# Fixed SBUF homes for the attention's queries, keys and values; the first batch loaded from the projection phase, in loads of 16 rows

## The reference, cut to what matters

```python
def _L0_attn_ref(x, Wqa, Wqb, Wkva, Wkvb, Wout, bout):   # after a layer norm; 8 batches of 512 tokens, 256 wide
    H, KVH = (16, 4)                                      # D = 16
    q = (x @ Wqa @ Wqb).reshape(b, s, H, D)
    kv = (x @ Wkva @ Wkvb).reshape(b, s, KVH, D, 2)
    k, v = (kv[..., 0], kv[..., 1])
    q, k = _rope(q), _rope(k)
    ...
    scores = jnp.einsum('bqhd,bkhd->bhqk', q, k) * scale  # k, v repeated over 4 heads; causal mask
    w = jax.nn.softmax(scores, axis=-1)
    out = jnp.einsum('bhqk,bkhd->bqhd', w, v).reshape(b, s, E)
    return out @ Wout + bout
x = x + _L0_attn_ref(_layernorm(x), ...)
x = x + _L0_xattn_ref(_layernorm(x), ctx_1024, ctx_1024, ...)   # 8 x 64 context rows, 16 heads of 64, and an MLP
x = x + _L0_ffn_ref(_layernorm(x), ...)                         # ternary weights
```

## Time and profile before

| | us |
|---|---|
| median of 3 runs | 1288.27 |
| lowest and highest | 1285.8, 1289.26 |
| the profiled execution | 1285.26 |
| its span, first to last instruction | 1283.3 |

### The profile page before, as it was taken

The page is one execution under the profiler, slowest core; times in us unless marked ns, Lnnn a source line. Parts: engine busy times, 40 slices in busy tenths (PEclk is TensorE's granted clock), DMA queues, the critical chain, the costliest instruction groups (busy, mean ns, idle before and its releaser), DMA issues. The chain is left out here.

```text
span 1283.3 us, 23288 instructions
## 1 busy us (share of the span) xinstructions
PE 1041.0 (81%) x7133; PEld 759.8 (59%) x7133; DVE 800.5 (62%) x1737; ACT 648.8 (51%) x1155; POOL 369.8 (29%) x516
## 2 busy tenths in 40 slices
PE   3777148888899997488257999999999999998997
PEld 2444013334444442478246787978878787886986
DVE  3888546567777772576246565656756565766554
ACT  1333205456666666455133647465564746546554
POOL 0333326567433333101031213122211222221110
PEclk9777658889999999699677999999999999999999
DMA  2332323334222210336711211212101121010000
GB/s 90 100 118 90 113 98 104 109 107 125 95 93 92 90 42 34 126 140 263 268 50 49 80 38 66 67 65 65 65 17 49 65 65 65 16 64 2 18 1 33
DMA packets 52994, 103.89 MB, mean 81 GB/s; under 512 B 6656, under 2 KB 32768, under 8 KB 48832
## 3 DMA queue, kind: packets, MB, share of 16 engines
q1 hardware_dynamic: 49756, 95.62, 22.0%
q0 software_dynamic: 1920, 6.03, 1.6%
q10 hardware_dynamic: 1252, 1.39, 0.4%
HBM read 63.05 MB, written 39.58 MB: 80 GB/s over the span
## 5 line engine op out<-in xcount | busy, mean ns | idle before, releaser
L803 ACT ACTIVATE p_probs<-p_psS 128x512 f32<-128x512 f32 (+1 forms) x352 | 181.0, 564 | 123.6 <-ACTq L802 121.3
L705 DVE CUSTOM_DVE_ANT_0 p_psA<-p_psA,p_mask 128x512 f32<-128x512 f32 (+1 forms) x256 | 155.6, 647 | 104.4 <-DVEq L703 104.1
L1856 DVE TENSOR_TENSOR p_hl<-p_h,p_hh 128x512 fp32r<-128x512 f32 x128 | 100.9, 791 | 119.9 <-DVEq L1855 119.0
L837 PE MATMUL p_psA<-p_ks,p_qs 96*128 96x512 bf16 (+3 forms) x512 | 144.7, 318 | 35.4 <-PEq L835 34.9
L1674 ACT ACTIVATE p_h<-p_psG,w_columns 128x512 f32<-128x512 f32 x128 | 88.2, 689 | 128.5 <-ACTq L1673 127.6
L856 PE MATMUL p_psS<-p_qs,p_ks 99*128 99x256 bf16 (+3 forms) x512 | 131.8, 311 | 21.2 <-PEq L881 12.3
L724 POOL TENSOR_SCALAR_AFFINE_SELECT p_probs<-p_probs 128x512 f32<-128x512 f32 x128 | 80.7, 634 | 133.1 <-POOLq L723 113.9
L867 PE MATMUL p_psO<-p_probs,p_v 128*32 128x512 f32 (+3 forms) x1024 | 93.3, 460 | 25.1 <-PEq L863 24.4
L2140 PE MATMUL p_psY<-p_n,p_hh 128*128 128x256 f32 x512 | 106.8, 292 | 7.9 <-PEq L2131 4.5
L856 PEld LDWEIGHTS p_psS<-p_qs,p_ks 99*128 99x128 bf16 x512 | 44.0, 99 | 107.9 <-issue 93.2
L2140 PEld LDWEIGHTS p_psY<-p_n,p_hh 128*128 128x128 f32 x512 | 86.2, 196 | 15.9 <-issue 14.7
(11 more groups left out here) (260 smaller groups left out, 2744.0 us busy)
## 6 DMA issues: line engine op xcount, KB each, us to landing
p_n<-n_parts SPq DMA_DIRECT2D x16, 1024.0 KB, 6.8
o_sums<-p_o SPq DMA_DIRECT2D x32, 256.0 KB, 3.0
n_parts<-p_nh SPq DMA_DIRECT2D x8, 1024.0 KB, 3.9
n_parts<-p_nl SPq DMA_DIRECT2D x8, 1024.0 KB, 6.1
q_parts<-p_part SPq DMA_DIRECT2D x48, 128.0 KB
p_qs<-q_parts SPq DMA_DIRECT2D x32, 192.0 KB
p_x<-in_x_dram SPq DMA_DIRECT2D x8, 512.0 KB, 4.2
p_qs<-q_parts SPq DMA_DIRECT2D x32, 128.0 KB
```

Source lines behind the costliest of these rows:

```text
L705: nc.vector.tensor_tensor_reduce(out=bank[:, 0:w], in0=bank[:, 0:w], in1=mask[:, S - w:S], scale=1.0, scalar=MASKED, op0=ALU.add, op1=ALU.max,
L803: nc.scalar.activation(probs[:, g % 2, at:at + n * w], psS[place(s, turn) % SB][:, 0:n * w], ACT.Exp, scale=SCALE).then_inc(exp_done, 1)
L837: last = nc.tensor.matmul(bank[:, z * w:(z + 1) * w], qs[0:SROWS, k, g * G + r0 + z, i * P:(i + 1) * P], ks[0:SROWS, k, g, 0:w], start=Tru ...
L1856: nc.vector.tensor_tensor(hl[:, s, :], h[:, s, :], hh[:, s, :].bitcast(F32), ALU.subtract).then_inc(h_parts, 1)
```

## The change

44 KB per partition of SBUF, three tensors, are allocated ahead of all phases: `home0` for `qs` (32 KB), `home1` for `ks` (8 KB), `home2` for `v` (4 KB). The later phases lay tiles of their own onto them (`nh`, `nl`, `k`, `k2` in the preparation; `q`, `rows`, `sq`, `o` in the mixing), instead of allocating them apart. In the profile of the changed kernel these tiles are all called `home`.

`load_queries` and `load_keys` are functions of the module. They issue one DMA for each of the six blocks of 16 rows, six where there were three, and none has a broadcast source. This holds for every load of the attention, not only the first.

In the projection, SP's stores of the third pair (`stores(B - 4 + k, k, True)`) are followed, unit by unit, by loads of batch 0 into the home: behind units 0 to 3 the queries of groups 0 to 3, behind units 4 and 5 the two halves of the keys and values. The phase ends with a wait for them. In the attention ACT raises the semaphores of the first batch by hand and loads the keys of the second batch alone; SP issues all queries of the second batch ahead of `maxima(0, 0)`.

```diff
+def load_queries(queue, scr, qs, b, k, g, landed):
+    heads = slice(g * G, (g + 1) * G)
+    for row, (pq, _) in enumerate(PAIRS):
+        queue.dma_start(qs[row * D:(row + 1) * D, k, heads, :].rearrange("p h t -> p (h t)"),
+                        scr["q"][pq, :, b, heads, :].rearrange("d h t -> d (h t)")).then_inc(landed, 16)
+
+def load_keys(queue, scr, ks, v, b, k, z, landed):
+    two = slice(z * KVH // 2, (z + 1) * KVH // 2)
+    for row, (_, pk) in enumerate(PAIRS):
+        queue.dma_start(ks[row * D:(row + 1) * D, k, two].rearrange("p g t -> p (g t)"),
+                        scr["k"][pk, b, :, two].rearrange("d g t -> d (g t)")).then_inc(landed, 16)
+    queue.dma_start(v[:, k, two].rearrange("p g t n -> p (g t n)"),
+                    scr["v"][b].rearrange("p (z n) -> p z n", z=2)[:, z]).then_inc(landed, 16)
...
+            def first_batch(n):
+                if n < KVH:
+                    load_queries(sp, scr, qs0, 0, 0, n, first_in)
+                else:
+                    load_keys(sp, scr, ks0, v0, 0, 0, n - KVH, first_in)
...
+                    if ahead:
+                        first_batch(n)
...
-                stores(B - 4 + k, k)
+                stores(B - 4 + k, k, True)
...
+            sp.wait_ge(first_in, 16 * (KVH * len(PAIRS) + 2 * (len(PAIRS) + 1)))
...
-                    if first and g + 1 < KVH:
-                        load_queries(1, 1, g + 1)
...
             for g in range(KVH):
-                load_queries(0, 0, g)
+                load_queries(sp, scr, qs, 1, 1, g, q_in[1][g])
             maxima(0, 0)
-            load_queries(1, 1, 0)
...
-            for k in range(2):
-                for z in range(2):
-                    load_keys(act, k, k, z)
+            for g in range(KVH):
+                act.sem_inc(q_in[0][g], 16 * len(PAIRS))
+            for z in range(2):
+                act.sem_inc(kv_in[0][z], 16 * (len(PAIRS) + 1))
+            for z in range(2):
+                load_keys(act, scr, ks, v, 1, 1, z, kv_in[1][z])
```

More of the change, by code:

```diff
@@ L204, in load, with stores @@
                 sp.dma_start(x[:, k], a["x"][b].rearrange("(t p) f -> p t f", p=P)).then_inc(x_in[k], 16)
-            def stores(b, k):
+            def first_batch(n):
[3 more added lines that the diff above has]
+                    load_keys(sp, scr, ks0, v0, 0, 0, n - KVH, first_in)
+            def stores(b, k, ahead=False):
                 sp.wait_ge(v_ready, 1)
@@ L608, in attend_phase @@
         block = ctx.enter_context(nc.Block())
-        def load_keys(queue, b, k, z):
-            two = slice(z * KVH // 2, (z + 1) * KVH // 2)
-            row = 0
-            for pq in range(PARTS):
-                n = sum(p == pq for p, _ in PAIRS)
-                rows = slice(row * D, (row + n) * D)
-                queue.dma_start(ks[rows, k, two].rearrange("p g t -> p (g t)"),
-                                scr["k"][0:n, b, :, two].rearrange("i d g t -> i d (g t)")).then_inc(kv_in[k][z], 16)
-                row += n
-            queue.dma_start(v[:, k, two].rearrange("p g t n -> p (g t n)"),
-                            scr["v"][b].rearrange("p (z n) -> p z n", z=2)[:, z]).then_inc(kv_in[k][z], 16)
         @block.sync
@@ L626, in _ @@
                 sp.dma_start(dst, src).then_inc(loaded, 16)
-            def load_queries(b, k, g):
-                heads = slice(g * G, (g + 1) * G)
-                row = 0
-                for pq in range(PARTS):
-                    n = sum(p == pq for p, _ in PAIRS)
-                    rows = slice(row * D, (row + n) * D)
-                    sp.dma_start(qs[rows, k, heads, :].rearrange("p h t -> p (h t)"),
-                                 scr["q"][pq, :, b, heads, :].rearrange("d h t -> d (h t)").unsqueeze(0).broadcast_to([n, D, G * S])
-                                 ).then_inc(q_in[k][g], 16)
-                    row += n
             def maxima(k, g):
@@ L1387, in _, with mix_phase @@
             pe.sem_inc(MN_free, -MN_BANKS)
-def mix_phase(nc, a, scr, w, out):
+def mix_phase(nc, a, scr, w, q, rows, sq, o, out):
     with ExitStack() as ctx:
@@ L1433, in mix_phase @@
         minus = signs[:, 0:1]
-        o = sb("o", [P, C, S], F32)
         oh, ol = sb("oh", [P, C, S], F32R), sb("ol", [P, C, S], F32R)
         xin = sb("xin", [P, TT, E], F32)
-        x1 = sb("x1", [P, TT, E], F32)
-        q0 = sb("q0", [P, TT, E], F32)
+        x1, q0, base, x1b = rows
         z = sb("z", [P, TT, E], F32)
-        base = sb("base", [P, TT, E], F32)
-        x1b = sb("x1b", [P, TT, E], F32)
         x2 = sb("x2", [P, TT, E], F32)
@@ L2296, in decoder_block @@
            "rden": dram("rden", [B, H, S]), "n": dram("n_parts", [B, 2, P, XT * E])}
-    project_phase(nc, a, scr)
     with ExitStack() as ctx:
+        homes = [ctx.enter_context(nc.sbuf_tensor(f"home{i}", [P, n], F32))[:, :]
+                 for i, n in enumerate((H * S, KVH * S, 2 * KVH * TT * 2 * D))]
+        qs = homes[0].bitcast(BF16).rearrange("p (k h t) -> p k h t", k=2, h=H)
+        ks = homes[1].bitcast(BF16).rearrange("p (k g t) -> p k g t", k=2, g=KVH)
+        v = homes[2].rearrange("p (k g t n) -> p k g t n", k=2, g=KVH, t=TT)
+        half = H * S // 2
+        nh, nl = (homes[0][:, i * half:(i + 1) * half].bitcast(F32R).rearrange("p (z t n) -> p z t n", t=XT, n=E)
+                  for i in range(2))
+        q = homes[0][:, 0:half].rearrange("p (t s) -> p t s", t=XT)
+        rows = [homes[0][:, half + i * half // 4:half + (i + 1) * half // 4].rearrange("p (t n) -> p t n", t=TT) for i in range(4)]
+        sq = homes[1].rearrange("p (i s) -> p i s", s=S)
+        k, k2 = homes[1].rearrange("p (i n) -> p i n", i=2), homes[2]
+        o = homes[2].rearrange("p (c t) -> p c t", c=C)
+        project_phase(nc, a, scr, qs, ks, v)
         w = mixing_weights(nc, ctx)
@@ L2304, in decoder_block @@
             cw = context_weights(nc, until_n)
-            attend_phase(nc, a, scr, split_list(a, w, cw), split_sems)
-            prepare_phase(nc, a, scr, w, cw)
-        mix_phase(nc, a, scr, w, out)
+            attend_phase(nc, a, scr, qs, ks, v, split_list(a, w, cw), split_sems)
+            prepare_phase(nc, a, scr, w, cw, nh, nl, k, k2)
+        mix_phase(nc, a, scr, w, q, rows, sq, o, out)
 def mixing_weights(nc, ctx):
```

29 lines of the change are left out of this document (11 added, 18 removed).

## The result

The changed kernel takes **1252.06 us** (median; 1251.53 to 1255.04), the kernel before 1287.94 beside it on the same chip: a ratio of 0.973, with a 95% interval of 0.971 to 0.975. The forecast was 1270 with a range down to 1259, so the sign was right and the gain was nearly twice what was forecast. The profiled execution has a span of 1249.7 us against 1283.3, 33.6 us less, where 18.4 were expected.

The account below looks back on a forecast made before the run. The prediction took SP's issuing to bound the projection's end and a DMA backlog on two engines to hold up the attention; 4.6 - 16.0 - 7.0 = -18.4 us gave 1266.9, stated as a 1270 us median, range 1259 to 1282.

Parts of the forecast that it names:

- 38 loads in the projection: End of projection: 19.0 us of SP issuing less 14.4 us idle, so the phase ends 4.6 us later (0.8 to 13.7).
- p: What one 16-row load costs SP, issue and gap: taken as 0.50 us, bounds 0.40 and 0.74.
- The start of the attention: First batch: no wait for maxima, DVE's fill late next, column scores at T + 23.9 instead of T + 39.9: 16.0 us gained.
- Later groups: Groups after the first column scores: less refill backlog, 5.1 us of waits, 1.3 of clock, 0.6 of shorter waits; 7.0 gained.
- bound of half the excess: Later groups: upper bound 14.2 us, half of the 28.4 us by which seventeen groups exceed the pitch without refills.
- more comes back: Rival for the later groups: clock and POOL's gaps both follow the backlog, 14.2 us gained there, 1263 us; chance 0.16.
- SP in the loop: Key refills in the attention loop: SP ends 1.2 us before the next maxima, so no cost while p stays under 0.55.
- Nothing: ACT's 14 loads instead of 16 at the start and the homes' changed addresses: no effect on time.
- The rival that SP becomes the bound: Projection and loop: SP's load issues delay both; at p = 0.74 18 us slower, 1306 us; chance 0.04.
- The prediction's sentence on sizes: Attention loads: 96 and 128 KB become 64 and keys become 32, against a page calling transfers under 64 KB descriptor-dominated.
- The loads don't spread: Rival for the attention: 16-row loads drain like the old ones, maxima again need 14.9 us, 1285 us; chance 0.05.

Follow-up runs that it names:

- the shape alone: Kernel before with every attention load of queries and keys as six 16-row DMAs; nothing loaded early, no shared homes: 1250.63 us, ratio 0.972.
- the merged loads: Changed kernel with pairs reordered, so a group's queries are three DMAs of 48, 32 and 16 rows without a broadcast; keys stay six: 1247.63 us, ratio 0.969.

## Why the prediction was wrong

Step by step, as the prediction has them.

1. **38 loads in the projection**: forecast +4.6, measured +5.6. The mechanism held, p was 0.46 instead of 0.50, and nearly all of SP's idle time was used up. The last stores are issued 4.9 us later (147.76 to 152.65), and the rest is the way from them to T, 4.8 instead of 4.1.

2. **The start of the attention**: column scores at T + 23.9 forecast, T + 24.9 measured, with no wait for the maxima, the fill late next, and the maxima issued at T + 18.6 instead of T + 17.4. The first maximum came at T + 9.2, 1.3 later than the forecast T + 7.95, because the fill itself ran 1.4 us later after T. That there are 14 idle engines to spread over was right. What was wrong is how much they carry: 380 GB/s was scaled up from two engines' 24 each, and sixteen moved 230 at a share of 0.99, 14 each. It did no harm here since the maxima had six microseconds of room; in the start without the early batch, where PE waits at a share of 1.05, it counts. The backlog of before was also not SP's twelve query loads alone, as the prediction has it: of the 146 packets between 186.0 and 191.6 us, 73 were SP's and 73 ACT's, whose key loads of the old shape were issued until 176.2.

3. **Later groups**: forecast -7.0 with bounds 0 and 14.2, measured **-24.2**, of which 23.0 lie in the first seventeen groups. This is the step that failed, and its bound failed with it. The rows above split the 23.0 by the prediction's own terms:

   | in the seventeen groups, us | before | after | difference | predicted |
   |---|---|---|---|---|
   | PE's waits for the rows of maxima (L881, now L885) | 7.7 | 2.8 | -4.9 | -5.7 |
   | PE's busy time, same matmuls (the granted clock) | 149.5 | 139.5 | **-10.0** | -1.3 |
   | PE's waits for masked tiles (L863, now L867) | 16.3 | 7.6 | **-8.7** | 0 |
   | PE's waits for ACT's tiles | 0.6 | 1.2 | +0.6 | 0 |

   What the prediction read from SP's rows, the maxima behind the backlog, it sized rightly. It put POOL's waits at nothing ("POOL's 3.02 us gap ahead of it stays"), with no reason but that they were POOL's, and the clock at 1.3 us, read from one stretch of 6.8 us; the 8.25 us at the lower level behind PE's wait of 8.34, a wait that it took away itself, are in no term. Its bound of half the excess has no reason beside it, other than "Part of that is POOL's". The excess itself, 28.4, holds the wait of 3.5 us at 241.43 twice, since one piece ends with that column score and the other begins with the issue of the maxima before it; from column score to column score (191.75 to 371.46) seventeen groups exceed the pitch by 24.8, and half of that is 12.4. The split was not far off: without POOL's weight pieces, 13.3 of the 24.3 us were gone, 55%. But POOL's share was late for the same reason as SP's. Its pieces wait for their own DMAs, and those were late whenever loads of the old shape were in the queues: the third row below, 5.6 us, was 5.8 and 5.5 in the two runs with old loads and is 4.0 and 3.8 in the changed kernel and with the shape alone. DMA issues of the kernel before, POOL's (KB each, median us from issue to landing):

```profile
p_stage<-in_L_xattn_wk_dram POOLq DMA_DIRECT2D x4, 256.0 KB, 6.1
p_stage<-in_L_xattn_wv_dram POOLq DMA_DIRECT2D x4, 256.0 KB, 5.7
p_stage<-in_L_xattn_w_dram POOLq DMA_DIRECT2D x4, 256.0 KB, 5.6
p_stage<-in_L_xattn_w_dram POOLq DMA_DIRECT2D x8, 128.0 KB, 4.2
```

   The same of the kernel after, and of the kernel before with the pieces behind the groups, where little else is queued (the last row):

```profile
p_stage<-in_L_xattn_wk_dram POOLq DMA_DIRECT2D x4, 256.0 KB, 3.2
p_stage<-in_L_xattn_wv_dram POOLq DMA_DIRECT2D x4, 256.0 KB, 3.9
p_stage<-in_L_xattn_w_dram POOLq DMA_DIRECT2D x4, 256.0 KB, 4.0
p_stage<-in_L_xattn_w_dram POOLq DMA_DIRECT2D x8, 128.0 KB, 3.0
...
p_stage<-in_L_xattn_w_dram POOLq DMA_DIRECT2D x8, 128.0 KB, 2.3
```

   POOL works in order, so a piece that waits keeps the next mask waiting, and PE's wait for the mask was read as POOL's own slowness. The rival "more comes back" named the right mechanism (clock and POOL's gaps both follow the backlog) and gave it 0.16, but took its size from the same half. Half of the excess comes back with the refills' shape and half with that of the first two batches' loads, and the run with old refills says which half is which. The refills' 10.5 us (162.04 - 151.50) are 8.7 of waits for masked tiles and 2.5 of clock, less 0.6 of waits for ACT's tiles; the other 12.4 (174.47 - 162.04) are 7.5 of clock and 4.9 of waits for maxima, and no wait for POOL. Not settled is how much the clock would have cost by itself: the idle stretches and the lower level came and went together in these runs, so they can't be taken apart.

4. **SP in the loop**: forecast nothing, with 1.2 us of room. Right: 0.86 us of room, p 0.455, and the maxima 9.09 apart.

5. **Nothing** for the homes and ACT's loads, and preparation and mixing as long as before: right, 774.4 us each.

The rival that SP becomes the bound needed p of 0.64; the slowest six loads of 16 rows took 0.57 each, once, and those in the loop 0.455. The prediction's sentence on sizes, beside this rival, misreads them: a group's queries were loads of 192, 128 and 64 KB and became 64, and the 96 and 64 KB are the keys', which became 32. "The loads don't spread" was wrong in both its parts.

**How many engines, and how large a transfer.** The DMA share was 0.12 and 0.13 while the copies and parts of the old shape drained, 0.99 with loads of 16 rows, and 0.94 with the merged loads, which have the old sizes and a slow dimension of 48, 32 or 16. The Trainium skill, DMA: Bandwidth & Descriptors, "Why a DMA increments its semaphore by 16 and not by 1", has the number of engines follow from the slowest dimension in just this way; the trace agrees, with those shares. Twelve loads of up to 192 KB in the old shape gave 1286.97 us, twenty-four of 64 KB 1252.06, and twelve of up to 192 KB in the merged one 1247.63. The Trainium skill, DMA: Bandwidth & Descriptors, "Bandwidth", asks for fewer and larger transfers; taken alone it pointed the wrong way for the 35 us that the spread was worth. Between loads of the same spread the larger ones gained 4.4 us at most, with intervals that overlap, and that came with a T 6.0 us sooner (151.47), for SP had twelve loads fewer to issue in the projection.

## What to carry to other kernels

Before counting bytes or issues, look at how many DMA engines a load can use: a stretch where a DMA is late and the DMA share is 0.13 means two busy engines of sixteen, and a source with a slow dimension of 2 or 3, by a broadcast or by parts, is the first suspect. When such a backlog went here, POOL's loads, which the change doesn't touch, landed sooner too, so an engine that waits for its own DMAs in the same stretch must not be set aside as an independent limit. Loads moved to an earlier phase paid here only when their landing was what was late, after a 3.5 us fill had been moved too.

## What the runs showed of the hardware

- A DMA of 12 KB, issued behind loads in the old shape, let PE go only 14.9 us and 14.4 us later; behind loads of 16 rows 6.3 us later (176.05 to 182.38), and PE was not waiting for it.
- SP's issue of loads in the old shape grew slower as more were issued: in the kernel before, five took 3.57 us and the whole row of twelve 17.96; with the old shape in the projection, three took 2.03 us at first and 5.08 later, where six of 16 rows took 2.77 to 3.41. That the backlog is what slows the issue is inferred.
- With the old shape on SP's refills alone, POOL's own loads of the mixing weights (256 KB) took 5.5 us in the median to land instead of 4.0, POOL waited 13.4 us for its loads instead of 0.8, and PE waited 8.7 us more for POOL's masks.
- Two busy engines moved 24 GB/s each, sixteen together 219 to 230 GB/s at a share near 1.0, 14 each. Scaling up from a few engines gave 380 and was wrong by two thirds.
- With all engines busy, the same query bytes issued in half the time, by loads of up to 192 KB instead of 64 (5.5 instead of 11.1 us), came with PE's first scores 3 us later after T: T + 12.6 and 12.8 in two kernels, T + 9.8 and 10.1 in two with loads of 16 rows.
